# Two attention stages, their engine loops written out: a fused three-stage block on one core

## The chip, the cores and the metric

The kernel runs on one core of one Trainium2 chip. The metric is the device time in microseconds; smaller is better. The core has a matrix engine (PE, with its weight loads shown apart as PEld), a vector engine (DVE), an activation engine (ACT), a general engine (POOL) and a queue engine (SP), each with its own stream of instructions. They meet only through semaphores.

## What is computed

For 32 sequences of 64 tokens of width 256, in float32:

```python
x = x + xattn(layernorm(x), ctx, ctx)   # 16 heads of width 16, 256 keys each sequence
x = x + attn(layernorm(x))              # 16 heads of width 64, causal, 64 keys
x = x + ffn(layernorm(x))               # 256 -> 1024 -> 256, int8 weights and int16 activations simulated
```

Cross attention applies no mask and no scaling; self attention divides the scores by 8. A float32 product is made from a high and a low part of each operand in three matmuls (high*high, low*high, high*low).

## The kernel before

The 2048 tokens are 16 tiles of 128 rows. Two tiles are a *quad* (four sequences; QUADS = 8). Cross attention is `cross_attention`, self attention `self_attention`, and both are built alike: each engine has a function `body(i, last)` that issues its whole share of quad i, and `steps(eng, body)` says for which i it is issued. In the kernel before, quads 0, 6 and 7 are written out, and quads 1 to 5 are one body inside a loop that runs on the engine (`Fori(1, 6)`), so that i is a register there. Semaphores only count upwards and are never reset, so that a wait in the loop compares with a value worked out from the register, while one in a written-out quad compares with a constant. There is no barrier at the loop's end: each engine turns back by itself, when it gets there.

The order of the work is written by hand. In cross attention a quad has 16 steps s. In each step PE issues the scores of step s+2 (`score`, L415), the transposes of the probabilities of step s (`turn`, L425), and in some steps a weighting by V (`weigh`, L443) or one of ten projections for the next quads (`project`, L59 to L61, list EVENTS). Of these, four matter here: Q at s=4; the first K projection of the even tile at s=2, which reads CS0; and that of the odd tile at s=11, which reads CS1 (CS0 and CS1 are the context's parts, high and low). What PE leaves in the banks is taken by ACT (high part) and DVE (low part): QSh by ACT, then QSl by DVE (L647).

On DVE a quad has, around s=3 and s=4, the copy of a turned tile (L680), the scaling `On` (L693, it waits for PE's `turn_o`, L454), the layer norm's statistics for two quads ahead (L660, L665, only where `two_ahead(i)`, so not in quads 6 and 7), and the row maximum (L675), for which the exponentials on ACT (L569) wait. Two quads ahead also are a load of context and its high part on ACT, and the layer norm's normalization on DVE (L670).

On POOL a quad of cross attention is

```python
ctx_low(0, 2 * i + 3)                                                   # CS0l, L339
if two_ahead(i): rstd_of(i + 2)                                         # L333, L335
restack_q(pool, qst_in[0], 0, EV0 + EV * i + 3, CHUNKS * (2 * i + 1))   # 12 DMAs; waits for QSl, then scores
ctx_low(1, 2 * i + 4)                                                   # CS1l, L339
restack_q(pool, qst_in[1], 1, EV0 + EV * i + 3, CHUNKS * (2 * i + 2))   # 12 DMAs; waits for the last scores of the quad
```

so that the twelve copies of Q (Qst, L272) stand ahead of the low part of the context, for which PE's K projections wait. SP has the copies of K (Kst, L281).

Self attention has no DMA inside its quads. POOL divides there (L896), DVE subtracts maxima and sums, and PE does everything else. The feed-forward stage is not touched by the diff.

Of the kernel before, what the change touches and what calls it, by code (L numbers as in the profile page):

```python
# [24 lines left out]
QUADS = TILES // 2  # L25
# [126 lines left out]
def cross_attention(nc, X, ident, identb, causal, half, x, ctxT, xwq, xwk, xwv, xwo,  # L152
# [12 lines left out]
    with ExitStack() as ctx:  # L165
# [79 lines left out]

        def steps(eng, body):

            body(0, False)
            with eng.Fori(1, QUADS - 2) as i:
                body(i, False)  # L250
            body(QUADS - 2, False)
            body(QUADS - 1, True)

        def two_ahead(i):

# [31 lines left out]
        def _(sp):  # L287
# [25 lines left out]
            def body(i, last):  # L313
                late = isinstance(i, int) and i == QUADS - 2
                if not last:
# [4 lines left out]
                    if late:  # L320
                        for m in range(1, 4):
                            load_later(m)

            steps(sp, body)

        @block.gpsimd
        def _(pool):
# [30 lines left out]
            def body(i, last):  # L358
# [4 lines left out]
                if not last:  # L363
                    restack_q(pool, qst_in[0], 0, EV0 + EV * i + 3, CHUNKS * (2 * i + 1))
                    ctx_low(1, 2 * i + 4)
                    restack_q(pool, qst_in[1], 1, EV0 + EV * i + 3, CHUNKS * (2 * i + 2))

            steps(pool, body)

        @block.tensor  # L370
        def _(pe):
# [111 lines left out]
            def body(i, last):  # L483
                first = isinstance(i, int) and i == 0
                for s in range(16):
# [12 lines left out]
                    if s == 15 or (s == 8 and not first):  # L498
                        project_out(2 * i + (s - 15) // 7)

            steps(pe, body)
            weigh(QUADS - 1, 12, True)
            keep_busy(pe, 5, pJ[0][:, :], identb, causal)
# [267 lines left out]
def self_attention(nc, X, ident, identb, causal, half, raw, raw_in, ffn, w_inT, w_out):  # L771
# [12 lines left out]
    with ExitStack() as ctx:  # L784
# [79 lines left out]

        def steps(eng, body):

            body(0, False)
            with eng.Fori(1, QUADS - 2) as i:
                body(i, False)
            body(QUADS - 2, False)  # L870
            body(QUADS - 1, True)

        def two_ahead(i):

# [12 lines left out]
        @block.gpsimd  # L887
        def _(pool):
            def rstd_of(n):
                rstd_of_quad(pool, vare, rstd, mv, half, n, ln_mv, ln_ve, ln_rs, waited)  # L890

            def divide(i, s):

                pool.wait_ge(inverted, 4 * i + s + 1)
                rows = Pr[s // 2][:, :, s % 2, :]
                pool.tensor_tensor(rows, rows, rinv[s][:, :].unsqueeze(2).to_broadcast([P, 8, SQ]), ALU.mult  # L896
                                   ).then_inc(weighted, 1)

            rstd_of(0)
            rstd_of(1)  # L900

            def body(i, last):
                for s in range(4):
                    divide(i, s)
                if two_ahead(i):
                    rstd_of(i + 2)
                if not (isinstance(i, int) and i == 0):
                    rstd_of_quad(pool, vare3, rstd3, mv3, half, i - 1, l3_mv, l3_ve, l3_rs, waited)

            steps(pool, body)  # L910

        @block.tensor
        def _(pe):
# [97 lines left out]
            def body(i, last):  # L1011

                held = [("K", 2, i), ("K", 3, i)] if isinstance(i, int) and i == 0 else [("K", 3, i), ("Y", 1, i - 1)]
                for kind, s, k in plan(last):
# [6 lines left out]
                    else:  # L1021
# [3 lines left out]
                        fill(k % 2, kind, s, quad)  # L1025

            steps(pe, body)

        def target(kind, part):
# [16 lines left out]
        def _(act):  # L1046
# [41 lines left out]
            def body(i, last):  # L1088
# [28 lines left out]
                fills("K", 2)  # L1117

            steps(act, body)

        @block.vector
# [541 lines left out]
```

## Time and profile before

| | |
|---|---|
| median of 3 runs | 662.55 us (661.47 to 662.77) |
| the profiled execution | 659.37 us, its span 657.6 us |
| mean granted clock of the matrix engine | 0.986 of full speed |
| busy in the span | PE 92%, PEld 79%, DVE 72%, ACT 59%, POOL 30% |
| instructions executed | 18502 |

The span is what the profile covers; the 1.8 us beside it are start and end. The rows below are of the profiled execution. The profiler does not count register work, waits, branches and the issuing of DMAs as busy.

### The profile page before, as it was taken

The numbers are of one execution on the slowest core, as the hardware profiler recorded it, in microseconds if no ns is written. First come the engines' busy times: TensorE is split into PE (matmuls) and PEld (weight loads), VectorE is DVE, ScalarE is ACT, GpSimd is POOL, SyncE is SP. The second block draws the span as 40 slices with busy tenths as digits, with TensorE's granted clock in tenths as the row PEclk, the third lists the DMA queues.
The fourth block names the chain that finished last, engine by engine and source line by source line (L and its number), as shares of the span: only waits on it lengthen the run. The fifth ranks groups of instructions, "written<-read, shape, count | busy, mean of one in ns | idle before, by whom it ended". The sixth has DMA issues, their size and how long they took to land. (4 is left out here: it accounts for less than half of the span.)

```text
span 657.6 us, 18502 instructions
## 1 busy us (share of the span) xinstructions
PE 606.4 (92%) x6776; PEld 517.4 (79%) x6776; DVE 470.8 (72%) x989; ACT 387.1 (59%) x1017; POOL 198.4 (30%) x308
## 2 busy tenths in 40 slices
PE   4689999999998999899999999999999999689997
PEld 2578989898987888776787888898989797544597
DVE  4268888888886887776789757566666656467797
ACT  3287888887876888875332424333333333367795
POOL 4625554646454555300110212121212112150000
PEclk9789999999998999999999999999999999999999
DMA  7876767676767677833000000000000000000012
GB/s 257 200 189 171 188 170 187 166 191 165 190 162 166 144 177 208 213 127 100 30 2 2 1 1 0 0 0 0 0 0 0 2 2 2 10 0 1 0 49 81
DMA packets 35597, 58.44 MB, mean 89 GB/s; under 512 B 6912, under 2 KB 15232, under 8 KB 35552
## 3 DMA queue, kind: packets, MB, share of 16 engines
q1 hardware_dynamic: 25008, 36.85, 21.8%
q0 software_dynamic: 5952, 12.20, 7.8%
q10 hardware_dynamic: 4592, 8.78, 4.7%
q8 instruction: 29, 0.48, 0.3%
q14 instruction: 16, 0.13, 0.1%
HBM read 17.96 MB, written 2.10 MB: 31 GB/s over the span
## 5 line engine op out<-in xcount | busy, mean ns | idle before, releaser
L569 ACT ACTIVATE Pr<-pS,nmax 128x256 f32<-128x256 f32 x256 | 120.1, 485 | 23.2 <-DVE nmax L675 20.3
L675 DVE TENSOR_REDUCE nmax<-pS 128x2 f32<-128x512 f32 x128 | 87.5, 685 | 20.0 <-PE pS L415 18.5
L896 POOL TENSOR_TENSOR a_Pr<-a_Pr,a_rinv 128x512 f32<-128x512 f32 x32 | 32.7, 1044 | 185.8 <-DVE a_rinv L1185 185.8
L272 POOL DMA_DIRECT2D Qst<-QSh x124 | 62.2, 505 | 77.2 <-PE pS L415 59.9
L425 PE MATMUL pT<-ident,Pr 128*128 128x128 f32 x512 | 78.1, 275 | 1.2 <-DVE wraw L680 1.1
L1065 ACT ACTIVATE a_Pr<-a_Pr 128x512 f32<-128x512 f32 x32 | 20.2, 631 | 76.0 <-DVE a_Pr L1177 76.0
L415 PE MATMUL pS<-Kst,Qst 96*128 96x256 f32 x256 | 58.1, 309 | 6.4 <-ACT Pr L569 6.2
L425 PEld LDWEIGHTS pT<-ident,Pr 128*128 128x128 f32 x512 | 59.6, 141 | 2.6 <-issue 2.2
L569 ACT ACTIVATION_READ_ACCUMULATOR Pr<-pS,nmax 128x1 f32 x256 | 55.3, 216 | 0.0
L415 PEld LDWEIGHTS pS<-Kst,Qst 96*128 96x128 f32 x256 | 40.0, 192 | 15.0 <-ACT Pr L569 7.6
L59 PE MATMUL a_pJ<-a_XTh,a_W1h 128*128 128x256 f32 x128 | 37.1, 290 | 2.5 <-DVE X L1198 1.6
L59 PE MATMUL a_pJ<-a_XTh,a_W0h 128*128 128x256 f32 x128 | 37.3, 292 | 1.1 <-DVE a_XTl L1161 0.8
L60 PE MATMUL a_pJ<-a_XTl,a_W1h 128*128 128x256 f32 x128 | 36.2, 283 | 0.0
L60 PE MATMUL a_pJ<-a_XTl,a_W0h 128*128 128x256 f32 x128 | 36.2, 283 | 0.0
L61 PE MATMUL a_pJ<-a_XTh,a_W0l 128*128 128x256 f32 x128 | 36.2, 283 | 0.0
L61 PE MATMUL a_pJ<-a_XTh,a_W1l 128*128 128x256 f32 x128 | 36.2, 283 | 0.0
L272 POOL DMA_DIRECT2D Qst<-QSl x62 | 30.8, 497 | 0.0
L576 ACT ACTIVATE wraw<-pT 128x512 f32<-128x512 f32 x32 | 19.3, 602 | 18.7 <-PE pT L425 18.6
L1198 DVE TENSOR_TENSOR X<-a_pJ,X 128x256 f32 (+1 forms) x16 | 6.8, 424 | 32.0 <-PE a_pJ L61 32.0
L1501 ACT ACTIVATE f_Hid<-f_bank,f_bias_in,f_h_step 128x512 f32<-128x512 f32 (+1 forms) x32 | 23.6, 785 | 8.1 <-PE f_bank L1455 7.2
L1175 DVE TENSOR_REDUCE a_rmax<-a_pS 128x8 f32<-128x512 f32 x32 | 22.1, 691 | 7.9 <-PE a_pS L966 6.2
L59 PEld LDWEIGHTS a_pJ<-a_XTh,a_W1h 128*128 128x128 f32 x128 | 24.5, 191 | 3.4 <-DVE X L1198 1.8
(285 smaller groups left out, 1987.7 us busy)
## 6 DMA issues: line engine op xcount, KB each, us to landing
Kst<-WO_ints SPq DMA_DIRECT2D x96, 128.0 KB, 4.1
CT<-ctxT ACTq DMA_DIRECT2D x16, 512.0 KB, 4.8
Kst<-KSh SPq DMA_DIRECT2D x62, 128.0 KB, 3.3
Qst<-QSh POOLq DMA_DIRECT2D x124, 64.0 KB, 3.4
Kst<-KSl SPq DMA_DIRECT2D x31, 128.0 KB, 3.6
Qst<-QSl POOLq DMA_DIRECT2D x62, 64.0 KB, 3.4
X<-x SPq DMA_DIRECT2D x4, 512.0 KB, 8.7
out<-X SPq DMA_DIRECT2D x8, 256.0 KB, 2.2
```

The costliest lines, as they stand in the source:

```text
L59: pe.matmul(out, wh, xh, start=(k == 0), stop=False)
L60: pe.matmul(out, wh, xl, start=False, stop=False)
L61: last = pe.matmul(out, wl, xh, start=False, stop=(k == n - 1))
L272: eng.dma_start(f32(Qst[par][32 * u:32 * u + 32, jj]), f32(QS[part][32 * jj:32 * jj + 32, par])).then_inc(done, 16)
L415: last = pe.matmul(pS[c % 2][:, t, :], Qst[par][:, j % 4, j // 4, b, :, :], Kst[par][:, j, CK * b:CK * b + CK], start=True, stop=True)
L425: last = pe.transpose(pT[s % 2][:, t, k, :], Pr[s % 2][:, t, P * k:P * k + P], ident[:, :])
L569: act.activation(Pr[c % 2][:, t, :], pS[c % 2][:, t, :], ACT.Exp, bias=nmax[c % 2][:, t:t + 1], accum_out=rsum[par][:, c // 4, 2 * (c % 4) ...
L675: dve.tensor_reduce(nmax[s % 2][:, :], pS[s % 2][:, :, :], AX.X, ALU.max, negate=True).then_inc(maxed, 1)
L896: pool.tensor_tensor(rows, rows, rinv[s][:, :].unsqueeze(2).to_broadcast([P, 8, SQ]), ALU.mult).then_inc(weighted, 1)
L1065: act.activation(rows, rows, ACT.Exp, scale=E ** -0.5).then_inc(exped, 1)
L1175: dve.tensor_reduce(rmax[:, :], scores, AX.X, ALU.max).then_inc(maxed, 1)
L1501: act.activation(Hid[:, f, tokens(g)], bank[f % HB][:, :], ACT.Gelu, bias=bias_in[:, f:f + 1], scale=h_step[:, f:f + 1]).then_inc(gelu_don ...
```

## The change

In both attention stages `steps` issues the body for i = 0 to 7 from a loop of the generating program, with i a constant; no engine loops there. Every instruction that computes or moves data stays, in the same order on each engine; register arithmetic, the move that starts a loop and the branches go, and waits on registers become waits on constants. The feed-forward stage keeps its own loop.

```diff
         def steps(eng, body):
-            body(0, False)
-            with eng.Fori(1, QUADS - 2) as i:
-                body(i, False)
-            body(QUADS - 2, False)
-            body(QUADS - 1, True)
+            for i in range(QUADS):
+                body(i, i == QUADS - 1)
```

The same edit stands in `cross_attention` and in `self_attention`.

## Rows read from the trace of the kernel before

**Rows 1.** The page's first part: busy us, share of the span, instructions.
```profile
PE 606.4 (92%) x6776; PEld 517.4 (79%) x6776; DVE 470.8 (72%) x989; ACT 387.1 (59%) x1017; POOL 198.4 (30%) x308
```

**Rows 2.** Windows of cross attention: length, each engine's busy time (instructions), PEclk, DMA share, GB/s.
```profile
97.45:129.94 32.49, 31.85 (x340) 28.50 (x336) 26.99 (x58) 27.41 (x91) 17.57 (x28) 1.00 0.73 177
...
194.95:231.72 36.77, 33.30 (x340) 29.55 (x336) 27.12 (x58) 27.54 (x91) 17.57 (x29) 0.95 0.65 156
231.72:263.72 32.00, 31.54 (x340) 28.49 (x336) 25.56 (x52) 27.41 (x91) 16.56 (x26) 1.00 0.76 193
```

**Rows 3.** Windows of self attention: one quad inside the loop, then quad 6.
```profile
392.16:424.19 32.03, 31.38 (x463) 28.14 (x458) 20.41 (x47) 11.51 (x26) 5.91 (x8) 1.00 0.00 0
520.28:552.30 32.02, 31.30 (x463) 28.18 (x457) 18.80 (x41) 11.51 (x26) 5.02 (x6) 1.00 0.01 2
```

**Rows 4.** PE's waits in quads 1 to 3 of cross attention: total us, times, longest.
```profile
PE pS L415 <- ACT Pr L569: 1.3, 3, 0.4
PE pT L425 <- DVE wraw L680: 0.7, 3, 0.2
...
PEld pJ L59 <- POOL CS0l L339: 0.5, 3, 0.2
```

**Rows 5.** Timeline of POOL and PEld, a quad in the loop: start, length, what, [idle before].
```profile
135.83 2.39 POOL L339 TENSOR_TENSOR CS0l<-CT,CS0h 128x1024 fp32r<-128x1024 f32 x1
...
138.27 0.19 PEld L59 LDWEIGHTS pJ<-CS0h,Wh 128*128 128x128 f32 x1 [0.16 <-POOL CS0l L339]
...
148.96 0.57 POOL L272 DMA_DIRECT2D Qst<-QSh  x1 [3.97 <-PE pS L415]
...
154.94 2.41 POOL L339 TENSOR_TENSOR CS1l<-CT,CS1h 128x1024 fp32r<-128x1024 f32 x1
...
157.46 0.19 PEld L59 LDWEIGHTS pJ<-CS1h,Wh 128*128 128x128 f32 x1
```

**Rows 6.** Timeline of ACT and DVE in the same quad of the loop.
```profile
141.70 0.68 DVE L680 COPY PT<-pT 128x512 f32<-128x512 f32 x1
142.35 0.42 DVE L693 TENSOR_TENSOR On<-pY,rinv 128x256 f32<-128x256 f32 x1
...
145.33 1.26 ACT L552 ACTIVATE QSh<-pJ,rows_of 128x512 fp32r<-128x512 f32 x2
...
146.79 1.41 DVE L647 SCALAR_TENSOR_TENSOR QSl<-pJ,rows_of,QSh 128x512 fp32r<-128x512 f32 x2 [1.21 <-ACT QSh L552]
```

**Rows 7.** Timelines in written-out quad 0, then (from 237) in quad 6.
```profile
44.37 0.68 DVE L680 COPY PT<-pT 128x512 f32<-128x512 f32 x1
44.97 0.42 DVE L660 BATCH_NORM_STATS2 stats<-X 128x6 f32<-128x256 f32 x1
...
47.57 1.26 ACT L552 ACTIVATE QSh<-pJ,rows_of 128x512 fp32r<-128x512 f32 x2
48.86 1.41 DVE L647 SCALAR_TENSOR_TENSOR QSl<-pJ,rows_of,QSh 128x512 fp32r<-128x512 f32 x2 [0.79 <-ACT QSh L552]
...
237.61 2.40 POOL L339 TENSOR_TENSOR CS0l<-CT,CS0h 128x1024 fp32r<-128x1024 f32 x1
240.13 0.19 PEld L59 LDWEIGHTS pJ<-CS0h,Wh 128*128 128x128 f32 x1 [0.25 <-DVE XTl L654]
...
247.96 1.41 DVE L647 SCALAR_TENSOR_TENSOR QSl<-pJ,rows_of,QSh 128x512 fp32r<-128x512 f32 x2 [0.77 <-ACT QSh L552]
250.06 0.51 POOL L272 DMA_DIRECT2D Qst<-QSh  x1 [10.04 <-DVE QSl L647]
```

**Rows 8.** Timelines of POOL and PE around the long quad.
```profile
198.87 0.98 POOL L272 DMA_DIRECT2D Qst<-QSh  x2 [2.92 <-issue]
...
206.18 0.80 PE L59 MATMUL pJ<-CS0h,Wh 128*128 128x512 f32 x1 [2.82 <-POOL CS0l L339]
```

**Rows 9.** DMA queues that carry instructions: packets, MB, share of 16 engines.
```profile
q8 instruction: 29, 0.48, 0.3%
q14 instruction: 16, 0.13, 0.1%
```

More of the change, by code:

```diff
@@ L865, in steps @@
         def steps(eng, body):
[L867 to L871, printed above, removed]
+            for i in range(QUADS):
+                body(i, i == QUADS - 1)
         def two_ahead(i):
```

## The prediction

> **What bounds the kernel now.** I read the page's head first [rows 1]: PE is busy in 92% of the span, so what the loop costs the other engines is worth nothing unless PE, or a wait of PE, feels it. Then I cut the two stages into quads with the view of windows, at instants that come once a quad: in cross attention the start of POOL's second group of Qst copies, in self attention POOL's first division. That view answers most of the question, because the kernel holds its own comparison: quads 1 to 5 loop, quad 6 is written out.
>
> In self attention a looped quad lasts 32.03 us and written-out quad 6 lasts 32.02 [rows 3], though quad 6 has six DVE instructions fewer. In cross attention a looped quad lasts 32.49 (the next two 32.51 and 32.50), and quad 6 lasts 32.00 [rows 2]. Quad 6 has six DVE instructions fewer there too (DVE busy 25.56 against 26.99), so that the 0.5 is no pure loop cost but a ceiling on it. The quad from 194.95 to 231.72 is 36.77; that is a stall of its own, below.
>
> Last I read waits and timelines of one looped cross quad. PE's waits are small but there [rows 4]: 0.4 a quad for the exponentials, 0.2 for DVE's copy of a turned tile, 0.2 for the low part of the context that POOL makes. The third says most. POOL starts the second Qst group at 129.94, ends CS0l at 135.83 + 2.39 = 138.22, and PE loads its weights at 138.27; it starts the first group at 148.96, ends CS1l at 154.94 + 2.41 = 157.35, and PE follows at 157.46 [rows 5]. Twice a quad PE starts within 0.05 and 0.11 us of POOL's end. So the quad is a ring: PE's last scores, POOL's 12 copies and CS0l, PE's K projection at s=2; then turned outputs, DVE, ACT, DVE again for QSl, POOL's 12 copies and CS1l, PE's K projection at s=11; then PE to the last scores. A latency gone from that ring shortens every quad; one gone elsewhere does not.
>
> **The change part by part.**
>
> *Branches, register sums, start of the loops.* Where their engine is ahead of its data they cost nothing: their cover is PE's queued matmuls and the waits of the others. Self attention shows the case [rows 3]: with all of it 32.03, without 32.02. Five looped quads: 0.05 us, taken as 0. The same holds for the loop's turn in cross attention. PE's views of the turn show no idle time, and POOL's twelve copies run across its own turn without a gap: I take 0, and bound it at 0.5 a quad with the rest.
>
> *Waits on registers, cross attention.* Where an instruction has several conditions, the register form puts register steps between a release and the start. I take the three that lie on the ring:
>
> - ACT's QSh to DVE's QSl. In the loop QSh ends at 145.33 + 1.26 = 146.59 and QSl starts at 146.79 [rows 6], 0.20 us. Written out it is 48.83 to 48.86, 0.03 us, in quad 0 [rows 7]. Saved: 0.16 (0.17 with the rounding of starts).
> - DVE's copy of a turned tile to On, which waits for PE's transposes: 141.70 to 142.35 in the loop, 0.65 [rows 6]. In quad 0, where the statistics follow such a copy directly, the next start is 0.60 after it (44.37 to 44.97) [rows 7]. Between 0 (PE's transposes hold On anyway) and 0.05 are saved; I take 0.05, since DVE's chain behind it, up to the maximum that ACT waits for, is dense.
> - DVE's QSl to POOL's first copy. In the loop QSl ends at 146.79 + 1.41 = 148.20 and the copy starts at 148.96, 0.76 us [rows 5, 6]; in quad 6 it is 249.37 to 250.06, 0.69 us [rows 7]. Saved: 0.07.
>
> Together 0.28 us. PE must be able to follow: in quad 6 its way from the K projection at s=2 was not held by POOL at s=11, and that quad is 0.5 shorter than the looped ones, so 0.28 fits under what PE can do.
>
> *What the written-out form adds.* PE's K projection at s=2 starts 0.05 us after CS0l in the loop [rows 5], but 0.12 after it in quad 6 (240.01 to 240.13) [rows 7], since a constant wait there stands as an instruction between. Cost: 0.07 a quad at most, 0 where PE has its work late anyway. I take 0.0 to 0.07, and 0.02 in the sum, since quad 6 as a whole is shorter in spite of it.
>
> Per looped cross quad 0.28 - 0.02 = 0.26; for the five quads 1 to 5 the sum is 1.3 us.
>
> *More code to fetch.* The instruction queues moved 0.48 + 0.13 = 0.61 MB in 45 packets [rows 9]. A looped cross quad has 340+336+58+91+28 = 853 counted instructions [rows 2], a self quad 463+458+47+26+8 = 1002 [rows 3]. Four more copies of each are 7420; the 15866 executed [rows 1] less these are about 8450 written now, 72 bytes for each, so that the change adds 0.53 MB, some 32 packets of 16.6 KB. One takes 0.003 x 16 x 657.6 / 29 = 1.09 us of one DMA engine; about 15 of them fall into cross attention, where the engines are 73% busy. That is 16 us of 16 engines x 130 us, 0.8%. Written-out quad 6 streams its code at 76% DMA share and is the shortest [rows 2]. I take 0; if that cover fails, one packet late stops an engine for 1.09 us or more.
>
> *The long quad.* POOL issues 6 + 12 Qst copies ahead of quad 0, 24 in each of quads 0 to 3, and 12 and 2 in quad 4; then comes the stall of 2.92 us [rows 8], after copy 128. PE then waits 2.82 us for CS0l, and its granted clock is 0.95 of full over the window [rows 2], that is between the levels of 2.4 and 1.2 GHz. That quad is 4.27 us longer than its neighbours. A count of exactly 128 copies issued reads like a ring of requests that is full, not like the loop: neither the first nor the last iteration, nor its turn. The change leaves the copies as they are, so that I keep the whole 4.27.
>
> The profiled execution is 659.37 with 657.6 of span and 1.8 around it: 659.37 - 1.3 = 658.1, a ratio of 0.9980. The profiled run lies 3.2 under the median; on the median of the runs shown 662.55 x 0.9980 = 661.2 us.
>
> **The rivals.**
>
> *All of the 0.5 is loop cost.* For it: quad 6 is the only full written-out quad at full clock, and it is 0.5 shorter. Against: it lacks the statistics, which stand on the ring just ahead of the maximum. It would give 5 x 0.5 = 2.5: 660.0. A stronger form is that jumps back are themselves exposed. If each of the eight jumps back (four a stage) cost PE one packet of 1.09 us, 8.7 us would go: 653.8. The rows show nothing of it: looped and written-out self quads differ by 0.01. The Trainium skill, "Runtime: NRT & Kernel Launch", section "Instruction fetch mechanics", says that a taken branch whose target is out of the fetched window stops the engine for a fetch, and that kernels therefore prefer full unrolling; it also gives PE a larger instruction memory than the others, and by that the bodies here may simply fit, which would agree with the trace. The stall after copy 128 may move or go too (4.27, to 657). Together a chance of 0.12.
>
> *The ring is held elsewhere.* If the waits for exponentials (0.4 a quad) or the POOL leg from the last scores to CS0l (129.94 to 138.22, unchanged, 0.07 dearer on PE) take up what the other leg gives, the gain is 0 to 0.9: 661.7 to 662.6. For it: two waits remain on PE beside POOL's. Against: quad 6 shows that PE can pass s=11 earlier, and its whole length is 32.00. Chance 0.18.
>
> *Slower: code arrives late.* Written-out quads need a new packet in each engine's stream all along. In the cross stage they queue behind Kst, Qst and CT on the same 16 engines, and PE needs most of them. If one a quad is late by its own 1.09 us, five cost 5.5, net 5.5 - 1.3 = +4.2: 666.8. It decides from three late packets on: 3 x 1.09 = 3.3 against 1.3 is +2.0, 664.6. The clock can add to it, as in the long quad, where 2.8 us of idle PE became 4.27. For it: twice the code. Against: quads 0, 6 and 7 of both stages and the whole feed-forward stage run like that now. Chance 0.18, with the small dearer waits on PE in it.
>
> *The change does what it says* in the code; that no engine feels it is the second rival.
>
> **How the numbers follow.** The forecast (gain 0.9 to 2.1) has 0.52, the rivals 0.12, 0.18 and 0.18. About 0.2%, that is 1.3 us, is what a measurement of this kernel can tell from no change, and my 1.3 lies right on it: of the 0.52 some 0.30 are faster and 0.22 the same, since what I may have missed on the ring are gains more often than losses. Faster 0.30 + 0.12 = 0.42; same 0.22 + 0.18 = 0.40; slower 0.18. The range reaches down to the first rival (660.0 and the spread of the runs, 0.7): 659.3; and up to 663.6, through no change and into the start of the late packets, one net microsecond. The forecast's own range is 660.4 to 661.7.
>
> **What would show it.** In the changed profile cross quads 1 to 3 should last 32.25 (not 32.0, not 32.5); QSl should start 0.03 after QSh in all of them, and the copy 0.69 after QSl; PE should still start K within 0.12 of POOL's end at s=2. Self quads stay at 32.0. The instruction queues should have some 75 packets and 1.1 MB. The 2.92 should stand after copy 128 again. Wrong would be: idle time put down to issue on PE, ACT or DVE at places that no semaphore explains (late code), or cross quads of 32.0 (the statistics did not matter).

## The result, and the profile after

The changed kernel takes 655.96 us (median of 5 runs, 654.58 to 657.63) against 661.47 us before (median of 5, 660.67 to 662.77): a ratio of 0.9912, with a 95% interval of 0.9889 to 0.9935. That is faster by 5.5 us, where I had forecast 1.3, and it lies under my whole range. In a second set of executions (after_again, below) the changed kernel had a ratio of only 0.9963 (0.9939 to 0.9987), with a wide spread; one of its executions took 1169.16 us in a slow state and enters no comparison. The profiled execution of the changed kernel is 655.99 us with a span of 654.2.

The page's first part, of the changed kernel. The same instructions compute as in [rows 1], and PE is busy for 607.3 us in place of 606.4: nothing was taken off PE. What went is idle time.

```profile
PE 607.3 (93%) x6776; PEld 518.7 (79%) x6776; DVE 469.8 (72%) x989; ACT 387.5 (59%) x1017; POOL 198.6 (30%) x308
```

Windows of the changed kernel, cross attention, cut at the same instants as [rows 2]: quad 2, the long quad, quad 6.

```profile
97.30:129.56 32.26, 31.82 (x340) 28.50 (x336) 26.89 (x58) 27.46 (x91) 17.64 (x28) 1.00 0.76 181
194.09:230.55 36.46, 33.13 (x340) 29.51 (x336) 27.05 (x58) 27.56 (x91) 17.62 (x29) 0.95 0.66 161
230.55:262.50 31.95, 31.51 (x340) 28.45 (x336) 25.50 (x52) 27.43 (x91) 16.54 (x26) 1.00 0.77 191
```

A quad that looped takes 32.26 us now, 0.23 less than in [rows 2]; the long one is still there. Quad 6, written out in both kernels, stays at 32.0 (31.95 here). In self attention nothing moved against [rows 3]:

```profile
388.19:420.21 32.02, 31.31 (x450) 28.18 (x449) 20.32 (x46) 11.52 (x25) 5.92 (x8) 1.00 0.01 2
516.29:548.31 32.02, 31.31 (x450) 28.18 (x449) 18.79 (x40) 11.52 (x25) 5.02 (x6) 1.00 0.01 2
```

The timelines of one cross quad of the changed kernel hold the steps of the ring, which answer to [rows 5, 6]; they are taken together here, from POOL, PEld, DVE, ACT, DVE and POOL:

```profile
135.48 2.38 POOL L336 TENSOR_TENSOR CS0l<-CT,CS0h 128x1024 fp32r<-128x1024 f32 x1
137.98 0.19 PEld L59 LDWEIGHTS pJ<-CS0h,Wh 128*128 128x128 f32 x1 [0.23 <-DVE XTl L651]
...
141.34 0.68 DVE L677 COPY PT<-pT 128x512 f32<-128x512 f32 x1
141.95 0.42 DVE L690 TENSOR_TENSOR On<-pY,rinv 128x256 f32<-128x256 f32 x1
...
144.88 1.26 ACT L549 ACTIVATE QSh<-pJ,rows_of 128x512 fp32r<-128x512 f32 x2
146.18 1.41 DVE L644 SCALAR_TENSOR_TENSOR QSl<-pJ,rows_of,QSh 128x512 fp32r<-128x512 f32 x2 [1.05 <-ACT QSh L549]
...
148.29 0.57 POOL L269 DMA_DIRECT2D Qst<-QSh  x1 [3.71 <-DVE QSl L644]
```

QSl starts 0.04 us after QSh ends (146.14), the copy 0.70 after QSl ends (147.59), On 0.61 after the start of the copy of a turned tile, and PE's weights 0.12 after CS0l (137.86). In the loop these were 0.20, 0.76, 0.65 and 0.05. The row of PE's weights names DVE's XTl as what it waited for, but XTl ended at 137.72, ahead of CS0l: the wait for CS0l is a semaphore instruction of its own in this form (it stands in the trace from 0.04 us after CS0l, for 0.05 us), and the view puts the idle time down to the wait that the weight load itself carries. The same label stands in quad 6 of [rows 7].

The instruction queues of the changed kernel, beside [rows 9], have 80 packets and 1.09 MB, against 45 and 0.61:

```profile
q8 instruction: 54, 0.88, 0.6%
q14 instruction: 26, 0.21, 0.1%
```

And POOL stalls after its 128th copy as in [rows 8]; PE waits 2.91 us for what follows it:

```profile
198.00 0.98 POOL L269 DMA_DIRECT2D Qst<-QSh  x2 [2.91 <-issue]
...
205.40 0.77 PE L59 MATMUL pJ<-CS0h,Wh 128*128 128x512 f32 x1 [2.91 <-POOL CS0l L336]
```

**Where the rest comes from.** The quads account for 1.5 us. To find the rest I laid the two traces side by side from one anchor to the next: the first exponentials of each quad on ACT. The profile of the kernel before on which the prediction stands was a short one (659.37 us); I therefore compare with the run before_again below, whose profiled execution is typical (661.42 us, span 659.6). Of the 5.43 us between it and the changed kernel's, quads 1 to 4 give 4 x (32.50 - 32.26) = 0.96, the long quad 36.99 - 36.46 = 0.53, and 3.79 lie in one place that the prediction never priced: the passage from self attention to feed-forward. From the first exponentials of self attention's last quad to the first gelu it takes 34.75 us before and 30.96 after. The remaining 0.15 is the sum of small pieces, none over 0.11. The 0.53 is less certain than the 0.96: the long quad was 36.76 in the first profile of the kernel before and 36.99 in before_again.

This is the passage in before_again's timeline (start, length, what, [idle before]):

```profile
570.10 0.34 SPq L1395 DMA_DIRECT2D f_bias_in<-b_in  x1
570.11 1.28 ACT L1484 ACT_TABLE_LOAD   x1 [4.60 <-PEq L784]
...
573.43 0.20 ACT L1484 ACTIVATE f_table<-f_bias_in 128x1 f32<-128x1 f32 x1 [2.04 <-DMA f_bias_in<-b_in]
573.54 1.00 ACT L1487 ACTIVATE f_WI<-f_bankb 128x1024 bf16<-128x1024 bf16 x1
...
574.60 0.62 PE L1420 MATMUL f_bankb<-identb,WIq 128*128 128x128 bf16 x8 [2.12 <-ACT f_WI L1487]
```

and the same instructions in the changed kernel:

```profile
568.54 0.34 SPq L1389 DMA_DIRECT2D f_bias_in<-b_in  x1
568.56 1.28 ACT L1478 ACT_TABLE_LOAD   x1 [4.59 <-PEq L781]
...
570.12 0.20 ACT L1478 ACTIVATE f_table<-f_bias_in 128x1 f32<-128x1 f32 x1 [0.28 <-DMA f_bias_in<-b_in]
570.23 1.01 ACT L1481 ACTIVATE f_WI<-f_bankb 128x1024 bf16<-128x1024 bf16 x1
...
571.29 0.62 PE L1414 MATMUL f_bankb<-identb,WIq 128*128 128x128 bf16 x8 [0.36 <-ACT f_WI L1481]
```

At the start of feed-forward SP issues a load of 4 KB, the bias f_bias_in. ACT's first instruction there, f_table (a gelu on it that brings the function's table in early), needs it, and so does everything behind it on ACT: the copy f_WI of turned weights, which frees the bank for which PE waits. The view of DMA issues gives the time from issue to landing, first in before_again, then in the changed kernel:

```profile
f_bias_in<-b_in SPq DMA_DIRECT2D x1, 4.0 KB, 3.3
```

```profile
f_bias_in<-b_in SPq DMA_DIRECT2D x1, 4.0 KB, 1.6
```

Before, the load lands 3.3 us after its issue and ACT is idle for 2.04; after, it lands in 1.6 us and ACT is idle for 0.28. PE then idles 2.12 or 0.36 us. And PE's clock follows: windows of before_again, then of the changed kernel (length, PE, PEld, DVE, ACT, POOL busy, granted clock, DMA share, GB/s).

```profile
570.00:575.00 5.00, 2.68 (x22) 1.56 (x24) 2.57 (x9) 2.40 (x3) 0.92 (x2) 1.00 0.12 32
575.00:577.00 2.00, 1.35 (x9) 0.34 (x5) 0.25 (x1) 1.02 (x1) 0.00 (x0) 0.66 0.00 0
577.00:579.00 2.00, 1.92 (x6) 1.07 (x7) 1.22 (x6) 0.00 (x0) 0.00 (x0) 0.50 0.00 0
579.00:581.00 2.00, 2.00 (x9) 1.25 (x8) 0.34 (x3) 0.00 (x0) 0.00 (x0) 0.50 0.00 0
581.00:583.00 2.00, 2.00 (x9) 1.27 (x9) 0.98 (x2) 1.19 (x2) 0.00 (x0) 0.64 0.00 0
```

```profile
568.46:573.46 5.00, 3.87 (x28) 1.90 (x28) 2.70 (x10) 3.42 (x4) 0.93 (x2) 1.00 0.16 30
573.46:575.46 2.00, 1.78 (x8) 0.80 (x8) 1.43 (x6) 0.00 (x0) 0.00 (x0) 1.00 0.00 0
575.46:577.46 2.00, 2.00 (x13) 1.41 (x14) 0.92 (x4) 1.09 (x2) 0.00 (x0) 1.00 0.00 0
```

PE is busy for 2.68 of the first 5 us before and for 3.87 after; then its clock falls to 0.50 (1.2 GHz) before, and stays at 2.4 GHz after. In the profile that I predicted from, the clock did not fall, and the passage took 32.67 us. So, compared over single profiles, the late load alone costs 32.67 - 30.96 = 1.7 us, and the clock that often falls after it another 34.75 - 32.67 = 2.1.

Why does the same 4 KB land later before? The trace's packet records show instruction packets that start just after the bias packets (these start 0.95 us after the issue): in before_again one of 16 KB at +0.96 us, which takes 1.25 us, and one of 8 KB at +1.09. In the changed kernel there is one of 16 KB at +1.22 and none of 8 KB.

The same records show what the page does to the load. The load is 128 packets of 32 bytes, and it has landed when the last of 16 semaphore signals is in. In before_again 120 of the packets start by +1.21 us and 15 of the signals come by 1.56. The other eight packets, one sixteenth of the load, start at +2.20 to +2.26, just as the 16 KB packet ends (0.96 + 1.25 = 2.21), and the sixteenth signal comes at 3.32. In the changed kernel all 128 packets have started by +1.21, ahead of its 16 KB page, and all 16 signals are in by 1.55. So one sixteenth of the load waited for the page to end, and the load is as late as its last sixteenth. That the two share one of the 16 DMA engines is an inference from this sixteenth; these records do not name the engine.

What moved the page is the theory that the experiments test: the code has another length, so its pages are fetched at other moments.

### The profile page after: what moved, and what is told of

Read it like the earlier page. It is cut to its first block and busy times, and to the rows that moved or that the text cites. A ratio compares the mean times of both kernels' runs of the same rounds, so it can differ in the third digit from the quotient of the medians.

```text
span 654.2 us, 17386 instructions
## 1 busy us (share of the span) xinstructions
PE 607.3 (93%) x6776; PEld 518.7 (79%) x6776; DVE 469.8 (72%) x989; ACT 387.5 (59%) x1017; POOL 198.6 (30%) x308
## 5 line engine op out<-in xcount | busy, mean ns | idle before, releaser
L1059 ACT ACTIVATE a_Pr<-a_Pr 128x512 f32<-128x512 f32 x32 | 20.2, 631 | 75.7 <-DVE a_Pr L1171 75.7
L1192 DVE TENSOR_TENSOR X<-a_pJ,X 128x256 f32<-128x256 f32 x16 | 6.8, 423 | 30.7 <-PE a_pJ L61 30.7
```

What stands on the lines that cost most here:

```text
L1059: act.activation(rows, rows, ACT.Exp, scale=E ** -0.5).then_inc(exped, 1)
```

## The experiments

Theory A is this last sentence: the passage got shorter because the place at which code is fetched moved, not because loops went. Its rivals are that the loops themselves (their end, or self attention's) lengthen the passage, and that chance did it. "Passage" is the stretch defined above; 20.2 us of it lie ahead of the bias load's issue in every kernel that issues it there. Each ratio is against the kernel before, executed beside the other on the same chip. There were three such sets, in which the kernel before had a median of 660.94 us (before_again, cross_only, self_only, cross_dve_pool), 661.12 (the two bias_early kernels, pe_code_shift, q_split) and 661.37 (cross_pe_act_sp, after_again, q_split_warm).

**before_again**: the kernel before, unchanged.

> The kernel before, once more, to see what one execution differs from the next by. Ratio 1.000 within 0.2%. The profile of before that was read (span 657.6) is shorter than any timed run of it less 1.8 (658.9 to 661.0). If the missing 2 us are a thing of single executions, the cross quads 1 to 3 are again 32.5 and the two or three microseconds appear elsewhere: at the first load of the feed-forward stage (f_bias_in, for which ACT waited 1.96 us), in the long quad, or at the start. If they are a thing of the loops, quads 1 to 3 vary.

Measured: 661.33 us, ratio 1.0003 (0.9986 to 1.002). Its profile is the one quoted above. It fixes the floor of what can be told, and shows that the first profile (passage 32.67, clock in full) was not the usual one.

**cross_only** and **self_only**: one half of the diff each. The edit is that of the diff ahead of the prediction, in `cross_attention` alone or in `self_attention` alone.

> Only cross attention is written out, self attention loops. The theory of the ring: the whole of the quads' gain is here: cross quads 1 to 3 are 32.26, self quads 32.02 as in all kernels, ratio 0.992 to 0.997 of before. Rival (the 5.5 us belong to both stages, or to the place of the code in memory): ratio about 0.996, half of what the whole change gives, and the load of f_bias_in is late again (2 us instead of 0.3).

> Only self attention is written out, cross attention loops. The ring: cross quads 1 to 3 stay at 32.50, self quads at 32.02, so 0 from the quads; a ratio of 1.000, or 0.997 if the load of f_bias_in, which stands right behind this stage, is early (0.3 us of wait instead of 1.96) as in the changed kernel. Rival (half of the gain is in this stage's own loop): 0.995 with shorter self quads.

Measured: cross_only 656.15 us, ratio 0.993 (0.9905 to 0.9955), quads 32.26, passage 31.02, f_bias_in in 1.6 us. self_only 657.13 us, ratio 0.9952 (0.9936 to 0.9969), cross quads 32.50, self quads 32.02, passage 33.12 in its profile (659.34 us, the slowest of its runs) with the clock at 0.51 in one window, f_bias_in in 2.4 us. Each half alone gives most of the gain, and the two do not add up. self_only gave more than was expected of it (1.000, or 0.997 with the load early). Self attention written out leaves every one of its quads as it was, and yet the total falls by 3.8 us (660.94 to 657.13; 3.2 by the ratio). A cost for each turn of a loop cannot do that; a moved coincidence can. Its profile shows only 34.75 - 33.12 = 1.6 us of it in the passage, since that execution lay 2.2 us over the median and had the clock fall there; of the remaining 2.2 us a full clock there could give the larger part, but no trace shows it.

**cross_dve_pool** and **cross_pe_act_sp**: cross attention written out on two engines, and on the other three.

```diff
-        def steps(eng, body):
+        def steps(eng, body, written_out=False):
+            if written_out:
+                for i in range(QUADS):
+                    body(i, i == QUADS - 1)
+                return
             ...
-            steps(dve, body)          # and steps(pool, body)
+            steps(dve, body, True)    # and steps(pool, body, True)
```

> In cross attention only DVE and POOL are written out; PE, ACT and SP keep their loop, and all of self attention does. The ring (QSh to QSl 0.16 sooner, the copy to On 0.05, QSl to POOL's copy 0.07): cross quads 1 to 3 are 32.2 to 32.3 as with all engines written out. Rival (PE's or ACT's own register steps were what held the quad): 32.4 to 32.5 here.

> The kernel before, with cross attention written out on PE, ACT and SP alone; DVE and POOL keep their loops (the complement of the run with only DVE and POOL written out). Theory A (the 0.24 us a quad come from waits on registers by DVE and POOL, whose copies stand on the ring; the rest from the place at which PE's instruction page is fetched): cross-attention quads at 32.5 us, as before, but PE's program is shifted as in the changed kernel, so f_bias_in lands in 1.6 us, the passage takes 31.0 us and the time is 656.5 to 658. Rival B (the shorter passage needs DVE or POOL out of their loops): passage 33 to 35 us, time 660.5 to 662. Rival F (PE's, ACT's or SP's waits on registers matter on the ring too): quads at 32.35 or less.

Measured: cross_dve_pool 658.37 us, ratio 0.9974 (0.9951 to 0.9998); cross_pe_act_sp 657.84 us, ratio 0.9955 (0.9933 to 0.9976). One quad of each, first with only DVE and POOL written out, then with only PE, ACT and SP:

```profile
97.50:129.76 32.26, 31.84 (x334) 28.54 (x333) 26.89 (x58) 27.47 (x91) 17.68 (x29) 1.00 0.73 180
```

```profile
100.58:133.18 32.60, 31.91 (x334) 28.51 (x333) 27.01 (x57) 27.46 (x89) 17.61 (x29) 1.00 0.73 179
```

This splits the gain. The ring's part (32.50 to 32.26) comes from DVE and POOL alone, as the three waits of the prediction say, since these are DVE's and POOL's. With them in the loop QSl again starts 0.19 us after QSh ends:

```profile
146.28 1.26 ACT L556 ACTIVATE QSh<-pJ,rows_of 128x512 fp32r<-128x512 f32 x2
...
147.73 1.41 DVE L651 SCALAR_TENSOR_TENSOR QSl<-pJ,rows_of,QSh 128x512 fp32r<-128x512 f32 x2 [1.21 <-ACT QSh L556]
```

The passage's part comes from the other three: 34.98 us, f_bias_in in 3.6 us, with PE, ACT and SP as before; 31.02 us, 1.6 us, with these written out, although no quad got shorter. With them the quads are even 0.10 longer than in the loop and than expected (32.60 against 32.50): PE's weights start 0.11 us after CS0l in place of 0.05, and the ring of DVE and POOL is as slow as before. The total of cross_pe_act_sp is within what was expected.

**bias_early_before** and **bias_early_after**: the two bias loads are issued at the head of self attention, before and after the change.

```diff
+            sp.dma_start(bias_in[:, :], b_in).then_inc(bi_in, 16)                    # self_attention
+            sp.dma_start(bias_out[:, :], b_out.partition_broadcast(P)).then_inc(bo_in, 16)
...
-            sp.dma_start(bias_in[:, :], b_in).then_inc(bi_in, 16)                    # feed_forward
-            sp.dma_start(bias_out[:, :], b_out.partition_broadcast(P)).then_inc(bo_in, 16)
```

> The kernel before, with the two bias loads of the feed-forward stage (f_bias_in and f_bias_out) issued at the head of self attention, some 180 us before they are used. Theory A (the passage between the stages lost 3.8 us because a 4 KB bias load landed late, behind instruction pages that were fetched at that moment, and the clock then fell): from the last self-attention quad's first exps to the first gelu 30.5 to 31.0 us in place of 34.75, the clock granted in full there, and 657.0 to 657.8 us (ratio 0.993 to 0.995). Rival B (the passage is shorter in the changed kernel for another reason, such as the state in which the loop left the engines): the passage stays at 32.5 to 35 us and the time at 660.5 to 662. The cross-attention quads stay at 32.50 us under both.

> The changed kernel with the same early bias loads. Theory A: its loads already landed in 1.6 us, so little is left: 655.2 to 656.0 us, and the distance to the kernel before with early loads is only what the ring of cross attention gives, 1.3 to 1.8 us. Rival B: the distance between the two stays near 5 us.

Measured: bias_early_before 656.70 us, ratio 0.9937 (0.9914 to 0.996); bias_early_after 655.25 us, ratio 0.9916 (0.9891 to 0.9942). The passage is 30.71 us in both, with the clock in full. Two moved lines give the looped kernel 4.4 us, and the whole change then adds 656.70 - 655.25 = 1.45, near what the five quads give. That figure is rough: the executions of the two overlap (656.31 to 658.73 against 653.92 to 657.10), and in their profiles the long quad is 37.00 us with a fall of the clock and 35.16 without. The first total is 0.3 us under what theory A expected, and the second is inside. The bank for which PE idled 2.12 us in before_again is free in bias_early_before when PE gets there; no wait stands beside the row:

```profile
572.31 0.62 PE L1421 MATMUL f_bankb<-identb,WIq 128*128 128x128 bf16 x8
```

This decides what the late load costs: take it out of the passage, and the loops cost about what the prediction said, and not the 5 us of the rival. It does not say why the load was late; the packet records and the next run do.

**pe_code_shift**: the kernel before, with 60 small matmuls in PE's idle time at the very start (11.3 to 14.3 us), so that PE's program is longer by some 120 instructions ahead of everything.

```diff
+                elif ahead == 0:
+                    for _ in range(60):
+                        pe.matmul(pO[:, 0, 0, 0, :], identb[:, :], causal[:, 0, :], start=True, stop=True, ...)
```

> The kernel before with 60 matmuls of 128x64 added on PE in its idle time at the very start (11.3 to 14.3 us), into a bank that is overwritten: PE's program is longer by some 120 instructions ahead of all stages, and the work of every stage is the same. Theory A with the page fetched for PE as the culprit: the instruction page of 16 KB is no longer fetched within a microsecond of the bias load, f_bias_in lands in 1.6 to 2.5 us in place of 3.2, and the time falls by 1.5 to 4 us to 657.5 to 660. If the page belongs to another engine (SP, which issues the load): landing 3.2, passage and time unchanged at 660.5 to 662. The start itself costs at most 0.3 us more.

Measured: 656.18 us, ratio 0.9932 (0.9909 to 0.9955), 1.3 us under the range expected. Loops, loads and stages are those of before; 550 us later the bias load lands in half the time, and the passage takes 31.02 us:

```profile
f_bias_in<-b_in SPq DMA_DIRECT2D x1, 4.0 KB, 1.6
```

The packet records show why: the 16 KB packet is now at -5.66 us, only the 8 KB one stands at +1.08, and all 128 packets of the load have started by +1.21. The gain beyond the 3.7 us of the passage is from the start of the kernel, which the added matmuls also change: its first exponentials come at 33.75 us in place of 35.61, with the clock in full from 16 to 22 us.

Laid side by side, from the profiles and their packet records (us after the bias load's issue; "last packet" is the start of the last of the load's 128; "clock" is the lowest of the 2 us windows between the load and the first gelu):

| kernel | 16 KB page | 8 KB page | last packet | f_bias_in lands in | passage | clock |
|---|---|---|---|---|---|---|
| before | +0.99 | +1.09 | +2.23 | 3.2 | 32.67 | 1.00 |
| before_again | +0.96 | +1.09 | +2.26 | 3.3 | 34.75 | 0.50 |
| cross_dve_pool | +1.03 | +1.09 | +2.53 | 3.6 | 34.98 | 0.50 |
| self_only | -5.00 | +1.06 | +1.66 | 2.4 | 33.12 | 0.51 |
| pe_code_shift | -5.66 | +1.08 | +1.21 | 1.6 | 31.02 | 1.00 |
| cross_only | +5.02 | +2.46 | +1.26 | 1.6 | 31.02 | 1.00 |
| cross_pe_act_sp | +5.05 | none | +1.25 | 1.6 | 31.02 | 1.00 |
| changed | +1.22 | none | +1.21 | 1.6 | 30.96 | 1.00 |

A 16 KB page within 0.1 us of the load's own packets goes with a landing of 3.2 to 3.6 us in all three profiles that have it, and none without it is over 2.4. The packets show the same picture each time. In the three, the first of the load's last eight packets starts within 0.02 us of the 16 KB page's end (2.19, 2.21 and 2.47), and the seven others follow it. In self_only eight packets start at +1.62 to +1.66, as the 8 KB page ends (1.62), and fifteen signals come by 1.57, the last at 2.44: there the smaller page held up one sixteenth. In pe_code_shift the 8 KB page stands at the same moment and holds up nothing, so that a page near in time is not enough; by the inference above it must also stand on the same DMA engine as a part of the load. Why the last signal comes 0.8 to 1.1 us after the last packet in these four late loads, and 0.4 in the others, is open.

**after_again**: the changed kernel once more.

> The changed kernel once more: 655.5 to 656.7 us, quads 32.26, passage 30.95. What is open is the long quad, 36.46 us in one profile and 35.15 us in that with early bias loads: if that difference is PE's clock, which falls to half in some executions after the stall on POOL, it is 36.2 to 36.8 with the clock at 0.50 in one stretch, or 35.15 with the clock in full.

Measured: 658.87 us in the median of the eleven executions compared, ratio 0.9963 (0.9939 to 0.9987). Its profiled execution is 655.48, quads 32.28 to 32.31 and passage 30.93, as expected. The median is a miss of 2.2 us: the runs compared reach from 655.24 to 662.23, and their mean granted clock from 0.992 down to 0.976, the longer ones with the lower clocks. The kernel before spreads as well, from 657.57 (0.989) to 664.21 (0.977) over the runs of these comparisons. The fastest execution of each, 654.58 and 657.57, differ by 3.0 us: that is close to the ring's 1.5 and the 1.7 of the late load at full clock. Where the changed kernel loses its clock in its slower executions no trace shows, since the profiled ones were short. The long quad is one place where it can. Its window here and in bias_early_after:

```profile
197.37:232.53 35.16, 31.82 (x334) 28.49 (x333) 27.07 (x57) 27.56 (x89) 19.01 (x31) 1.00 0.69 166
```

```profile
196.26:231.42 35.16, 31.82 (x334) 28.53 (x333) 27.07 (x57) 27.56 (x91) 19.00 (x31) 1.00 0.69 166
```

35.16 is 32.26 and the stall of 2.9; the changed kernel's first profile had 36.46 with the clock at 0.95 over the window. So 1.3 of that quad's excess of 4.2 was clock.

**q_split**: the changed kernel with early bias loads, and with part of POOL's Qst copies issued by SP: half of those of one buffer, a quarter of the other's. POOL issues 123 in all in place of 186.

```diff
+                    restack_q(sp, qst_sync[0], 0, EV0 + EV * i + 3, CHUNKS * (2 * i + 1), (0, 1))     # SP
+                    restack_q(sp, qst_sync[1], 1, EV0 + EV * i + 3, CHUNKS * (2 * i + 2), (0,))
-                    restack_q(pool, qst_in[0], 0, EV0 + EV * i + 3, CHUNKS * (2 * i + 1))             # POOL
-                    restack_q(pool, qst_in[1], 1, EV0 + EV * i + 3, CHUNKS * (2 * i + 2))
+                    restack_q(pool, qst_in[0], 0, EV0 + EV * i + 3, CHUNKS * (2 * i + 1), (2, 3))
+                    restack_q(pool, qst_in[1], 1, EV0 + EV * i + 3, CHUNKS * (2 * i + 2), (1, 2, 3))
```

> The changed kernel with early bias loads, and with half of the Qst copies of the one buffer and a quarter of those of the other moved from POOL to SP, so that POOL issues fewer than 128 of them in all. Theory C (the long quad waits on POOL, which stalls 2.9 us at an issue after 128 of its copies): no stall of that length on POOL, the long quad falls from 36.5 to 32.3 to 33 us, and 650.5 to 652 us. Rival D (the stall has another cause, such as the point in the stage): it stays, the time is 654 to 657 us. Rival E: SP's queue, which also carries the Kst copies, now delivers Q or K later, each quad grows by 0.5 us or more and the time is above 656.

Measured: 650.43 us, ratio 0.984 (0.9816 to 0.9865), the fastest version but for the next, with which it is level, and 0.1 us under the range expected. Quad 2 and what was the long quad:

```profile
98.53:130.59 32.06, 31.49 (x334) 28.45 (x333) 26.88 (x57) 27.42 (x91) 13.11 (x20) 1.00 0.74 182
194.85:227.08 32.23, 31.49 (x334) 28.46 (x333) 26.87 (x57) 27.42 (x90) 13.10 (x20) 1.00 0.73 181
```

The stall is gone and the quad is 32.23 us; against bias_early_after's 35.16 that is 2.9 us, and 0.2 us more come off each other quad, since POOL's leg of the ring is shorter: PE's weights at s=2 start 1.07 us after CS0l, so POOL no longer holds them. The runs lie within 2.0 us, where bias_early_after's spread over 3.2. That the count decides and not the moment is supported, not proven: in all eleven profiles here in which POOL issues the 186 copies the halt, of 2.91 or 2.92 us, stands after the 128th, but it stands near the same instant too (197.0 to 199.9 us), and the copies moved to SP lighten POOL's queue in both respects.

**q_split_warm**: the same with the 60 matmuls of pe_code_shift.

> The version with early bias loads and the Qst copies shared between POOL and SP, with the 60 idle-time matmuls at the start as well. If the 1.6 us that the start gained in the run with the 60 matmuls is the clock (granted in full from 16 to 22 us, where it was 0.50 before): first exps at 33.7 in place of 35.3 us, and 648.5 to 649.3 us. If it was chance: 650.4, as without them.

Measured: 650.19 us, ratio 0.9832 (0.9801 to 0.9864). The clock at the start is as expected, first q_split_warm, then q_split:

```profile
16.00:18.00 2.00, 1.81 (x15) 1.84 (x16) 0.97 (x5) 0.96 (x1) 0.69 (x2) 1.00 0.99 255
18.00:20.00 2.00, 1.28 (x11) 1.08 (x9) 0.71 (x2) 1.64 (x4) 0.25 (x1) 1.00 1.00 232
```

```profile
16.00:18.00 2.00, 1.90 (x9) 1.93 (x10) 0.88 (x4) 1.05 (x1) 0.78 (x2) 0.50 1.01 257
18.00:20.00 2.00, 2.00 (x15) 2.00 (x15) 0.00 (x0) 0.97 (x3) 0.15 (x1) 0.74 1.03 231
```

but the total is not: I had expected 648.5 to 649.3. The first exponentials come at 34.24 in place of 35.28, and two cross quads of this profile took 32.53 and 32.32 in place of 32.05 and 32.05. The two versions can't be told apart.

## Why the prediction was right and wrong

- **Branches, register sums, start of the loops: 0.** Right. Self quads are 32.03 and 32.02 us in the two forms, and cross_pe_act_sp, without the loops of PE, ACT and SP, has no shorter quad (32.60).
- **The three waits on the ring: 0.28 a quad.** Right, one by one: 0.20 to 0.04, 0.65 to 0.61, 0.76 to 0.70, together 0.26. cross_dve_pool shows that the quads' whole gain lies in the code of DVE and POOL; the three waits were not changed one at a time.
- **The dearer wait on PE: 0.02, up to 0.07.** Its 0.12 us after CS0l appeared; the quad as a whole is 32.26 where 32.25 was said. Where nothing on the ring got shorter (cross_pe_act_sp) the quad grew by 0.10, of which this wait explains 0.07 at most; the rest is open. Over the five quads 1.5 us in the profiles and 1.45 in the pair with early loads, against the 1.3 of the sum.
- **The long quad: all of its excess kept.** Right for the stall (2.91 against 2.92). What I took as one number was two: 2.9 of stall and 1.3 to 1.6 of clock, and the second is not there in every execution.
- **More code to fetch: 0.** This is the step that failed. The term was put at 0, and what it should have held measured 3.8 us in the passage: 1.7 for the load that no longer lands late, 2.1 for the clock that no longer falls after it. Its size was right (80 packets and 1.09 MB, for about 75 and 1.1), and so was the finding that no page stops an engine in the quads, which buries the rival of late code. What failed is the reading of it: I asked only whether a page comes late to its own engine, and whether the DMA engines have room on average. A page can also stand in the way of somebody else's small load, and for that its moment counts, not the number of pages. With the kernel before the 16 KB page met the one load of the program on which ACT and PE wait with nothing else to do, and held up one sixteenth of it; five of the six other layouts of the code in the table did not have that meeting. I cut only the attention stages into windows, since the change lies there, and had no term for the passage behind them. Its rows were in the trace: ACT idle for 2.0 us on a load of 4 KB that took 3.2.
- **The base.** I noted that the profiled execution lay 3.2 under the median and scaled it. Against the median of five, 661.47, it lies 2.1 under, and that is the size of the clock's fall in the passage (32.67 against 34.75), a cost that the typical execution had and my rows did not show.
- **The rivals.** "All of the 0.5 is loop cost" falls (32.26, not 32.0). "The ring is held elsewhere" falls. "Jumps back are exposed", under which 653.8 came out near the time measured, falls too, and shows how a right number can come from a wrong cause: self_only removes four of the eight jumps back and no quad of it changes. The Trainium skill, "Runtime: NRT & Kernel Launch", section "Instruction fetch mechanics", calls the crossing of a 16 KiB boundary mostly hidden. For the engines that run the code the traces agree (self quads of 32.03 and 32.02 us). That passage says nothing of a data load beside the page, and there the cost shows: a landing of 3.3 us in place of 1.6.

What stays open: where the rest of self_only's 3.8 us is; why pages near in time hold up a part of the load in one kernel and not in another; which engine's program the 16 KB page belongs to (shifting PE's moved it, which points to PE); and where the changed kernel loses its clock in its slower executions, with which its gain is between 0.4% and 0.9%.

## What to carry to other kernels

When an edit changes only the length of the code, look for the places where an engine waits for one small load with nothing queued behind it, above all the first instructions of a stage, and see which instruction packets stand beside that load; such a load belongs a stage earlier. Cut the whole program into stretches, not only the stage that is edited, and profile the kernel before twice, since one lucky clock hides what the typical execution pays. A total that agrees with a theory is no support for it until the stretch that changed is the one the theory names.

## What the runs showed that I had not expected

- 60 idle-time matmuls in the first 15 us make a load 550 us later land in 1.6 in place of 3.3 us, by moving an instruction page. The kernel is 4.9 us faster; in its profile 3.7 are in the passage and 1.9 at the start, where the clock was higher.
- A load is as late as its last sixteenth: with a 16 KB page beside it, eight of 128 packets started 1.0 us after the others and the landing went from 1.6 to 3.3 us.
- After an idle stretch of 2.1 us on PE, in 5 us of which it was busy for 2.68, the clock fell to 0.50 for some 7 us in before_again, and the passage was 2.1 us longer than in the first profile of the same program, in which the clock did not fall.
- POOL's issue of copies halts for 2.9 us after 128 of them, whatever the form of the code, and does not when it issues 123: 2.9 us, and with the clock's fall behind it, which is not in every execution, 4.2 us.
